# GpSimd multiplies two tiles of h by C in one instruction

## The reference

```python
delta = jax.nn.softplus(dt @ dt_w.T + dt_b)
A = -jnp.exp(A_log)
deltaA = jnp.exp(jnp.einsum('bld,dn->bldn', delta, A))
deltaBu = jnp.einsum('bld,bln->bldn', delta * xc, Bm)
def step(h, inp):
    dA, dBu, c = inp
    h = dA * h + dBu
    y = jnp.einsum('bdn,bn->bd', h, c)
    return (h, y)
```

## Time and profile before

| | |
|---|---|
| median of 3 runs | 3500.1 us (3485.4 to 3516.8) |
| span of the profiled execution | 3515.5 us |
| PE busy | 3302.5 us, 94% |
| DVE busy | 2910.4 us, 83% |
| ACT busy | 2743.3 us, 78% |
| POOL busy | 1476.2 us, 42% |

### The profile page before, as it was taken

One profiled execution on the slowest core, in us unless ns is written; L12 is line 12 of the kernel. 1 busy time (PEld: TensorE's weight loads), 2 busy tenths in 40 slices (PEclk: granted clock), 3 DMA queues, 4 the chain that ended last, 5 costly groups with the idle time before them and its releaser, 6 DMA issues. The chain is left out here.

```text
span 3515.5 us, 72417 instructions
## 1 busy us (share of the span) xinstructions
PE 3302.5 (94%) x25249; PEld 2130.5 (61%) x25249; DVE 2910.4 (83%) x2827; ACT 2743.3 (78%) x4665; POOL 1476.2 (42%) x1379
## 2 busy tenths in 40 slices
PE   7699999999999999977999999999999999988798
PEld 4333333333333333335788888888888888876565
DVE  2689999889989999733599999999999999999322
ACT  2168888878878888832799999999899999998344
POOL 3100000000000000000588899898888899899200
PEclk9779999999989999978999999999999999999999
DMA  5430202020211200032111111111111111112431
GB/s 175 111 39 5 41 5 41 7 39 15 32 24 22 36 10 5 5 88 99 37 50 62 66 61 67 64 55 66 53 58 67 61 61 61 57 48 94 136 114 54
DMA packets 94140, 192.57 MB, mean 55 GB/s; under 512 B 16805, under 2 KB 31941, under 8 KB 92297
## 3 DMA queue, kind: packets, MB, share of 16 engines
q1 hardware_dynamic: 82616, 174.28, 18.0%
q10 hardware_dynamic: 9680, 9.84, 0.9%
q0 software_dynamic: 1536, 4.20, 0.6%
HBM read 136.64 MB, written 51.12 MB: 53 GB/s over the span
## 5 line engine op out<-in xcount | busy, mean ns | idle before, releaser
L1215 POOL TENSOR_TENSOR m_g<-m_hs,m_cb 128x512 f32<-128x512 f32 x1024 | 1303.8, 1294 | 194.9 <-PE m_ps_y L1247 87.7
L575 DVE TENSOR_REDUCE a_mx<-a_ps_m 128x2 f32<-128x1024 f32 x1024 | 1242.5, 1224 | 92.9 <-PE a_ps_m L433 73.1
L551 ACT ACTIVATE a_probs<-a_ps_s 128x512 f32<-128x512 f32 x2048 | 1110.6, 596 | 207.4 <-PE a_ps_s L463 156.4
L1347 DVE TENSOR_TENSOR_SCAN m_hs<-m_da,m_carry,m_ps_x 128x512 f32<-128x512 f32 x768 | 938.5, 1262 | 41.4 <-PE m_ps_x L1235 33.1
L433 PE MATMUL a_ps_m<-a_k,a_q 48*128 48x512 f32 x2048 | 773.2, 470 | 34.5 <-DMA a_q<-q_scr 20.0
L463 PE MATMUL a_ps_s<-a_q,a_k 50*128 50x512 f32 x2048 | 773.0, 458 | 12.9 <-issue 5.6
L1307 ACT ACTIVATE m_da<-m_delta,m_a_cur 128x512 f32<-128x512 f32 x1024 | 716.1, 713 | 0.2
L470 PE MATMUL a_ps_o<-a_probs,a_v 128*32 128x256 f32 x8192 | 669.4, 399 | 11.7 <-ACT a_o L538 8.3
L1235 PE MATMUL m_ps_x<-m_ident,m_bu 128*128 128x128 f32 x4096 | 628.5, 276 | 50.0 <-DVE m_hs L1347 35.6
L1292 ACT ACTIVATE m_bu<-m_dut,m_bt 128x512 f32<-128x512 f32 x832 | 593.3, 714 | 67.1 <-PE m_ps_x L1235 67.0
L1247 PE MATMUL m_ps_y<-m_ident,m_g 128*128 128x128 f32 x4096 | 618.0, 274 | 0.6 <-POOL m_g L1215 0.6
(11 more groups left out here) (142 smaller groups left out, 2405.8 us busy)
## 6 DMA issues: line engine op xcount, KB each, us to landing
m_cb<-c_scr SPq DMA_DIRECT2D x128, 512.0 KB, 3.7
y_scr<-m_ysb SPq DMA_DIRECT2D x16, 1024.0 KB, 6.6
ffn_y<-y_scr SPq DMA_DIRECT2D x14, 1024.0 KB, 7.3
a_k<-k_scr SPq DMA_DIRECT2D x96, 128.0 KB, 6.7
a_q<-q_scr SPq DMA_DIRECT2D x96, 128.0 KB, 9.2
q_scr<-p_partsq SPq DMA_DIRECT2D x16, 512.0 KB, 3.3
k_scr<-p_partsk SPq DMA_DIRECT2D x16, 512.0 KB, 3.3
m_xn<-xn_scr SPq DMA_DIRECT2D x16, 512.0 KB, 4.9
```

What stands on the lines that cost most here:

```text
L551: nc.scalar.activation(probs[:, t % PR, HEADS[j]], turned(i), ACT.Exp, scale=float(DK) ** -0.5).then_inc(exped, 1)
L575: nc.vector.reduce_max(mx[:, i:i + wide], ps_m[:, b:b + wide], AX.X).then_inc(m_maxed, 1)
L1215: nc.gpsimd.tensor_tensor(g[:, t % NG], hs[:, t % NHS], cb[:, quarter % 2, n % CQ], ALU.mult).then_inc(g_ok, 1)
L1347: nc.vector.tensor_tensor_scan(hs[:, t % NHS, rev], da[:, t % NDA, rev], ps_x[:, t % NX, rev], carry[:, n, i:i + 1] if p else 0.0, ALU.mul ...
```

## The change

GpSimd's loop goes over the odd tiles alone. One instruction multiplies the two tiles t-1 and t of `hs`, which lie side by side in the ring, by the same row of C (given twice by a step of zero), into two neighbouring products, and adds 2 to `g_ok`. It waits for both scans. The ring of products has six buffers instead of five, so that pairs fall on whole pairs of buffers; the memory comes from the ring of decays, eight instead of nine. The first two `du` products of the next step are made behind tile 13 instead of 12, since the loop only stops at odd tiles.

```diff
-NDA, NHS, NG, NBU = 9, 8, 5, 3
+NDA, NHS, NG, NBU = 8, 8, 6, 3
...
-        DU_AT = {12: (0, 1), 19: (2, 3)}
+        DU_AT = {13: (0, 1), 19: (2, 3)}
...
-                for t in range(LAST):
+                for t in range(1, LAST, 2):
                     s, k = divmod(t, TILES)
                     n = k // ND
                     quarter = s * (DS // CQ) + n // CQ
-                    if k % (CQ * ND) == 0:
+                    if k % (CQ * ND) == 1:
                         pool.wait_ge(c_in[quarter % 2], 16 * (quarter // 2 + 1))
                     if t >= NG:
                         pool.wait_ge(summed, t - NG + 1)
                     pool.wait_ge(h_ok, t + 1)
-                    nc.gpsimd.tensor_tensor(g[:, t % NG], hs[:, t % NHS], cb[:, quarter % 2, n % CQ], ALU.mult).then_inc(g_ok, 1)
+                    pair = t % NHS - 1
+                    nc.gpsimd.tensor_tensor(g[:, t % NG - 1:t % NG + 1], hs[:, pair:pair + 2],
+                                            cb[:, quarter % 2, n % CQ:n % CQ + 1].to_broadcast([P, 2, CH]), ALU.mult).then_inc(g_ok, 2)
```

## The result

Fifteen runs of each kernel gave 3529.4 us with the change (median; 3503.5 to 3547.4) against 3505.6 before (3484.0 to 3526.7). The two medians are 24 us apart. The ratio on record is 1.0086, with a 95% interval from 1.0065 to 1.0107, which is some 30 us: slower, where I had forecast 7. The profiled execution has a span of 3516.6 us; that of before had 3515.5. The two spans say less than the steps do, for two reasons. That of before holds the 4.93 us multiply, which made one of its steps 103.4 us long. And its recurrence began at 1701.0 us, where that of the change began at 1688.4: the code ahead of it is the same in both, but TensorE's granted clock was at its lower level there for 201 us before and for 178 us with the change.

The account below looks back on a forecast made before the run. PE and DVE were taken to bound the kernel in turn. At +0.7 us a step, 14 steps gave +10, the last step -3 and step 0 nothing: +7 on 3500.1, forecast 3507 us, range 3475 to 3565.

Parts of the forecast that it names:

- The sign: Whole kernel: slightly slower, +7 us on the median of 3500.1, with positive and negative terms nearly cancelling.
- The race at its start: Behind scans of tile 4m+1: DVE's multiply starts 0.22 us before the pair released by the same scan, so is not blocked.
- the second rival: Multiply loses to the pair released by the same scan: 2.9 us at about ten places, 3640 us; chance 0.06.
- First rival: Multiply meets longer GpSimd locks at any phase: 100 us more waiting, +60 us, 3560; chance 0.17.
- the walk: Step 6 followed place by place where DVE's multiply meets GpSimd's pairs and du products: +0.7 us a full step.
- Together -1.3: Tiles 41, 49, 53, 57: shorter multiply waits save -0.44, about -0.35 let through, -0.15 and -0.39 us a step.
- I cost this at nothing: Ring of eight decays instead of nine: ScalarE idled only 0.2 us before its 1024 decays, so cost 0.
- the wait of 88 us for PE's reading: GpSimd's idle time before products while PE read an old one, ring of five: goes with six buffers.
- The product's idle time before PE's adds near zero: Expected in the profile after: GpSimd's products no longer wait for PE's reading, 88 us before.
- The fourth rival: Ring of six or du blocks starve PE, waiting for products of tiles 20 to 24: 3523 us; chance 0.10.
- 14 steps have all of it: The cost of +0.7 us a full step applies to 14 steps: +10 us.
- the last -3: Last step, without side matmuls or du: its 12 multiplies fall from about 0.8 to 0.55, -3 us.

## Why the prediction was right and wrong

**Right.** The sign, and the range of 3475 to 3565. The duration of the pair (2.37 for 2.37) from the slope between two lengths. The race at its start: the multiply released by the same scan was ahead everywhere, and no place shows the 2.9 us of the second rival. Tile by tile, the multiply's waits; at tile 5 the end of the scan behind moved by 0.89 (+0.86 said), at tiles 17 to 20 by 0.59 and back by 0.60 (0 said), at tile 22 by 0.51 (+0.45), at tile 26 by 0.94 and back by 0.25 (+0.7), at tile 33 by -1.08 and back by 1.09 (0). First rival: the four places of the walk got longer (5, 17, 21 and 25, which I had counted as five), and no other; the median multiply is 0.56, not 1.5.

**"Together -1.3" at tiles 41, 49, 53 and 57 is the term that was mis-sized.** The multiplies shortened by 1.7 us there, and the step by 0.5. After each of them the scan ran up to PE's side matmuls, at tiles 45, 52, 56 and 60, and the transposes behind these gave the time back. I had allowed for this behind tile 49 alone, and had read the other places in the profile of before, where DVE's waits hid how near PE was: in that stretch PE is busy for 32.36 of 32.44 us. The experiment with a lighter PE shows the step keeping most of it. With -0.5 in place of -1.3 a step costs +1.5 and not +0.7, which is what was measured: over 13 steps 10 us more.

**What had no term: the ring of products.** "I cost this at nothing" was said of the decays; the wait of 88 us for PE's reading I took as one that goes without effect. Without the pair, the rings take 0.95 us a step, since products that start earlier are out of the multiply's way earlier. In the kernel with the change, whose walk I did with the rings in it, this gain is already inside the durations; so the sum isn't wrong by it, but what I took for a change near zero is a pairing that costs 2.5 us a step and a ring that gives 1.

**"The product's idle time before PE's adds near zero" was right, but the row that I named does not show it.** From the waits with the change:

```profile
POOL m_g L1216 <- DVE m_hs L1349: 197.1, 219, 32.5
POOL m_g L1216 <- PE m_ps_y L1249: 81.0, 66, 3.1
```

It says 81 us where 88 were. The longest of the 66, in the timeline:

```profile
2201.20 2.36 POOL L1216 TENSOR_TENSOR m_g<-m_hs,m_cb 128x1024 f32<-128x1024 f32 x1 [3.10 <-PE m_ps_y L1249]
```

```profile
2198.30 3.61 DVE L1349 TENSOR_TENSOR_SCAN m_hs<-m_da,m_carry,m_ps_x 128x512 f32<-128x512 f32 x3
```

This pair multiplies the first two of the three scans, and the second ended at 2200.74: of the 3.10 us no more than 0.5 can be PE's. A wait for two semaphores is put down as a whole to one of them. Counted from the end of the second scan, the median pair starts 0.17 us behind it at every tile where GpSimd is free, and all pairs together are late by 2 us, for 94 before. The fourth rival had the other half of this: PE waited for products, up to 3250 us,

```profile
PE m_ps_y L1249 <- POOL m_g L1216: 0.7, 1, 0.7
```

once, for 0.7 us.

**"14 steps have all of it", the last -3, step 0 at 0: partly wrong.** Steps 0, 14 and 15 are shorter by 1.6, 2.1 and 1.4 us; 13 steps and not 14 have the cost.

**What the sum had no term for is the clock.** Behind the longer stall at tile 5 two of the half-clock spells last 6.8 us instead of one, and the steps that hold one reach 102.1. The five spells of steps 1 to 13 cost the change some 11 us, at 1.6 and 3.2 each.

**How far the account goes.** Of the two profiled executions: the medians of the steps, 99.54 and 97.96, give 13 x 1.58 = 20.5 us. Steps 1 to 13 of the change are 7.0 us in all above their median, through the steps with spells; those of before, the one with the 4.93 us multiply left out, are 3.3 above theirs: +3.7. Steps 0, 14 and 15 give back 5.1. That makes 19, and the stages differ by 13.7, since the 4.93 us multiply adds 5.4 to the one before. Timed were 24 by the medians and 30 by the ratio, with an interval from 23 to 38. The profiled execution of the change, at 3518.4 us and a clock of 0.967, is the fourth fastest of its fifteen runs, and the span of that of before lies among the slower of its own; so this pair of executions shows less than the typical one. The line of time against clock suggests that the rest goes with the lower clock of the other runs of the change; one execution of each can't say in which stage they lost it.

## The version that beats both

The multiply without the lock, on the loop and rings of before: 3464.9 us, 0.990 of before (0.987 to 0.993), and 0.982 of the change by the two ratios. If PE is the bound at 96.9 us a step, as argued above, what would come next is PE's side work.

## What to carry to other kernels

Where a shared lock couples two engines, merging two instructions of the one saves it time that may be off the path, and makes each race that the other engine loses nearly twice as dear. Walk the second engine's instructions through one period and ask at each who starts first; then ask who bounds the stretch in which a wait gets shorter, because a saving there is kept only as far as the next engine is behind. What helped most here was to take the instruction out of the race, even in a form that is slower when undisturbed.

## What the runs showed of the hardware

- The multiply with a sum took 722 ns in the mean (709 to 743) and its read 83 ns for 128 x 512 in fp32, at all 192 places, where the form without took 454 ns at best and up to 4930.
- Between two GpSimd instructions that follow one another, the multiply mostly got in or not by about 0.1 us. In the trace of before it waited for the next GpSimd instruction in all ten cases where that started 0.11 us or less behind the multiply's start. Where that was 0.12 or more it went first in all but three; these three lost although the next one came 0.50 to 0.90 us later, and why is open. One of them is the 4.93 us multiply of tile 21 in step 8: it stood behind two du products and two products in a row.
- A multiply that is first makes the product it meets longer: the pair 2.43 instead of 2.37.
- Spells of half the clock lasted 3.4 or 6.8 us in steps 1 to 13. With the change they came behind stalls of PE of about 1.7 us in two pieces, in five steps of 13 and not in the other eight, with the same work. One of 3.4 us made a step 1.6 to 1.7 us longer, one of 6.8 us 3.2.
